# Row turns ahead of the projection's product groups, two chunks of the feed-forward interleaved, and an earlier fetch of tile ends

## What is computed

```python
agg = jax.ops.segment_sum(w[:, :, None] * v[srcidx], tgt, num_segments=n)
attn = agg.reshape(n, D) @ Wo[l].T + bo[l]
x = _batchnorm(x + attn, g1[l], beta1[l])
ff = jax.nn.relu(x @ W1[l].T + b1[l]) @ W2[l].T + b2[l]
x = _batchnorm(x + ff, g2[l], beta2[l])
```

## Time and profile before

| | us |
|---|---|
| median of 3 runs | 3085.25 |
| lowest and highest | 3076.72 and 3087.95 |
| span of the profiled execution | 3095.6 |
| PE busy in it | 2657.9 (86%) |
| DVE busy in it | 1629.2 (53%) |
| granted clock of PE, mean | 0.938 |

### The profile page before, as it was taken

The page is one execution under the profiler, slowest core; times in us unless marked ns, Lnnn a source line. Parts: engine busy times, 40 slices in busy tenths (PEclk is TensorE's granted clock), DMA queues, the critical chain, the costliest instruction groups (busy, mean ns, idle before and its releaser), DMA issues.

```text
span 3095.6 us, 78344 instructions
## 1 busy us (share of the span) xinstructions
PE 2657.9 (86%) x32605; PEld 2143.5 (69%) x32605; DVE 1629.2 (53%) x3272; ACT 1321.1 (43%) x3690; POOL 1115.8 (36%) x1130
## 2 busy tenths in 40 slices
PE   5999997999999999758899788888888678599998
PEld 4877885777777777546488577777777465477777
DVE  5236785555555555456512355555554645656553
ACT  3324443555555555422232255555555322333432
POOL 0000002666666666400001267777777111222110
PEclk8999998999999999979999899999999889799998
DMA  5642003988899998641024489999999431122211
GB/s 195 228 175 107 31 28 140 317 313 316 309 331 322 317 325 297 222 121 41 14 97 154 160 321 354 352 349 347 350 347 352 126 113 57 38 89 92 69 59 58
DMA packets 231795, 621.75 MB, mean 201 GB/s; under 512 B 39008, under 2 KB 45792, under 8 KB 231427
## 3 DMA queue, kind: packets, MB, share of 16 engines
q0 software_dynamic: 137088, 466.78, 42.2%
q1 hardware_dynamic: 94339, 149.78, 14.6%
HBM read 538.80 MB, written 103.39 MB: 207 GB/s over the span
## 4 chain that ended last, share of the span: by engine, by line
PE 60%; DMA 16%; DVE 8%; POOL 7%; issue 6%; ACT 2%; SPq 0%; DVEq 0%; POOLq 0%; ACTq 0%
PE ps L1179 6%; DMA Y<-KVd,srcE 5%; PE ps L574 5%; PE ps L575 4%; PE ps L576 4%; DMA aggd<-stage,segs 4%; PE ps L1222 4%; PE ps L1209 4%; PE ps L774 3%; POOL Y L1096 3%; PE ps L942 2%; PE ps L944 2%; PE ps L943 2%; PE ps L1186 2%; PE ps L1872 2%
## 5 line engine op out<-in xcount | busy, mean ns | idle before, releaser
L1096 POOL DMA_INDIRECT Y<-KVd,srcE x449 | 430.2, 958 | 230.6 <-issue 115.8
L1370 ACT ACTIVATE stage<-ps,stage 128x128 f32<-128x128 f32 x832 | 294.8, 366 | 115.3 <-PE ps L1186 112.4
L1096 POOL DMA_INDIRECT WA<-KVd,srcE x186 | 179.3, 964 | 361.8 <-PE ps L576 268.1
L1351 ACT ACTIVATE work<-ps 128x512 f32<-128x512 f32 x309 | 179.8, 597 | 303.8 <-PE ps L1179 303.5
L1179 PE MATMUL ps<-ident,Y 128*128 128x128 f32 x1796 | 252.2, 280 | 32.2 <-DMA Y<-KVd,srcE 26.8
L1351 ACT ACTIVATE G<-ps 128x512 f32<-128x512 f32 x315 | 181.8, 597 | 223.5 <-PE ps L1179 223.1
L1277 DVE COPY G<-ps 128x512 f32<-128x512 f32 x208 | 143.8, 691 | 245.8 <-PE ps L1186 243.0
L574 PE MATMUL ps<-Wh,xs 128*128 128x512 f32 x600 | 238.7, 398 | 31.2 <-DVE xs L514 31.2
L1179 PEld LDWEIGHTS ps<-ident,Y 128*128 128x128 f32 x1796 | 199.2, 143 | 70.5 <-issue 49.3
L575 PE MATMUL ps<-Wl,xs 128*128 128x512 f32 x600 | 236.9, 395 | 0.0
L576 PE MATMUL ps<-Wh,xs 128*128 128x512 f32 x600 | 236.5, 394 | 0.0
(11 more groups left out here) (383 smaller groups left out, 6775.2 us busy)
## 6 DMA issues: line engine op xcount, KB each, us to landing
KVd<-stage SPq DMA_DIRECT2D x96, 256.0 KB, 2.0
aggd<-work SPq DMA_DIRECT2D x6, 2048.0 KB, 7.4
Qd<-stage SPq DMA_DIRECT2D x48, 256.0 KB, 2.0
G<-aggd SPq DMA_DIRECT2D x48, 256.0 KB, 2.7
Y<-KVd,srcE POOLq DMA_INDIRECT x449
Y<-in_x SPq DMA_DIRECT2D x4, 1536.0 KB, 14.7
G<-mixq SPq DMA_DIRECT2D x24, 256.0 KB
mixd<-rowsb SPq DMA_DIRECT2D x24, 256.0 KB
```

Of the source, the lines that this page charges most:

```text
L1096: pool.indirect_dma_start(out=kvs[a], out_offset=None, in_=KVd[l][:, :], in_offset=bass.IndirectOffsetOnAxis(ap=srcE[:, n:n + 1], axis=0)) ...
L1351: act.activation(kT[n % len(kT)], banks(l)[place_of(l, "k", n) % len(banks(l))][:, :], ACT.Copy).then_inc(out_a, 1)
L1370: last = act.activation(pT[g % len(pT)][:, P * i:P * (i + 1)], SC[g % 2][:, P * i:P * (i + 1)], ACT.Exp, bias=smin[:, t:t + 1], scale=-1.0 ...
```

## The change

In the output projection the turn of a row of the next chunk, and its low part on DVE, stand ahead of a product group and no longer behind it. In the feed-forward PE's order becomes the list `FF_ORDER`: hidden layer 0, then for each chunk the first output block, the hidden layer of the next chunk, and the other three output blocks; the banks follow that list. The fetch of the tile ends waits only for the last use of the buffer that it overwrites (slot 18 in the first layer, 0 in the second), and the wait for the end of the edge phase comes behind it.

```diff
+        ENDS_KV = (18, 0)
+
         def ends_sp(l):
-            edges_done(sp, l)
+            a = ENDS_KV[l]
+            sp.wait_ge(agg, NQ * l + (KVN[l] * (uses(ET, KVN[l], a) - 1) + a) // 4 + 1)
...
             sp.dma_start(ends, src).then_inc(ends_in, 16)
+            edges_done(sp, l)
...
+        FF_ORDER = [(0, 0)]
+        for c in range(NCK):
+            FF_ORDER += [(c, 1), (c + 1, 0)] if c + 1 < NCK else [(c, 1)]
+            FF_ORDER += [(c, i) for i in range(2, 5)]
+
+        def ff_bank(c, i):
+            return FF_ORDER.index((c, i)) % 4
...
                 for f in range(4):
+                    if c + 1 < NCK and f < len(NODE_TILES[c + 1]):
+                        turn_row(NODE_TILES[c + 1][f])
                     if c:
...
                     mm.then_inc(wo_mm, 1)
-                    if c + 1 < NCK and f < len(NODE_TILES[c + 1]):
-                        turn_row(NODE_TILES[c + 1][f])
...
+            for c, i in FF_ORDER:
+                c0, cn = CHUNKS[c]
+                bank, o = PS[ff_bank(c, i)], FF_ORDER.index((c, i)) - 4
+                if o < 0:
+                    pe.wait_ge(wo_add, WO * (l + 1))
+                else:
+                    before, part = FF_ORDER[o]
+                    if part == 0:
+                        pe.wait_ge(relu, NCK * l + before + 1)
                     else:
+                        pe.wait_ge(ff_add, WO * l + 4 * before + part)
+                if i == 0:
+                    is_normal(pe, 2 * l, c)
...
                     i = WO * l + 4 * c + f + 1
+                    if c + 1 < NCK and f < len(NODE_TILES[c + 1]):
+                        low_row(NODE_TILES[c + 1][f])
                     dve.wait_ge(wo_mm, i)
...
                     dve.bn_stats(out=st4[:, f, c, :], in_=xT[:, f, c0:c0 + cn]).then_inc(*step_v.up())
-                    if c + 1 < NCK and f < len(NODE_TILES[c + 1]):
-                        low_row(NODE_TILES[c + 1][f])
```

More of the change, by code:

```diff
@@ L1875, in finish_pe @@
                     mm.then_inc(wo_mm, 1)
-                    if c + 1 < NCK and f < len(NODE_TILES[c + 1]):
-                        turn_row(NODE_TILES[c + 1][f])
[L1878 to L1885, removed]
-                    else:
[L1887 to L1897, removed]
+            for c, i in FF_ORDER:
[7 more added lines that the diff above has]
+                        pe.wait_ge(relu, NCK * l + before + 1)
+                    else:
+                        pe.wait_ge(ff_add, WO * l + 4 * before + part)
+                if i == 0:
+                    is_normal(pe, 2 * l, c)
+                    for k in range(4):
+                        mm = pe.matmul(bank[:, 0:cn], W1[:, k, :], xT[:, k, c0:c0 + cn], start=(k == 0), stop=(k == 3))
+                    mm.then_inc(w1_mm, 1)
+                else:
+                    if i == 1:
+                        pe.wait_ge(relu, NCK * l + c + 1)
+                    pe.matmul(bank[:, 0:cn], W2[:, (i - 1) * P:i * P], work[:, c % 3, 0:cn], start=True, stop=True
+                              ).then_inc(w2_mm, 1)
         def finish_act(l, meanwhile, beside_ff):
@@ L1926, in finish_act @@
                     act.wait_ge(w2_mm, WO * l + 4 * (c - 2))
-                act.activation(work[:, c % 3, 0:cn], PS[5 * c % 4][:, 0:cn], ACT.Relu, bias=vec[:, C_B1 + l:C_B1 + l + 1]
+                act.activation(work[:, c % 3, 0:cn], PS[ff_bank(c, 0)][:, 0:cn], ACT.Relu, bias=vec[:, C_B1 + l:C_B1 + l + 1]
                                ).then_inc(relu, 1)
@@ L1997, in finish_dve @@
                         is_normal(dve, 2 * l, c)
-                    dve.scalar_tensor_tensor(out=xT[:, f, c0:c0 + cn], in0=PS[(5 * c + f + 1) % 4][:, 0:cn],
+                    dve.scalar_tensor_tensor(out=xT[:, f, c0:c0 + cn], in0=PS[ff_bank(c, f + 1)][:, 0:cn],
                                              scalar=vec[:, C_B2 + 4 * l + f:C_B2 + 4 * l + f + 1],
```

## The result

The changed kernel has a median of 3097.37 us over 15 runs (3085.58 to 3110.6), the kernel before 3081.19 us over 15 (3074.69 to 3093.23). The ratio is 1.0049, 95% interval 1.0036 to 1.0063: 15 us slower, between 11 and 19. The prediction said 3097, or 11.4 us more, in a range from 3083 to 3107. That 3097 and 3097.37 all but agree is partly luck: the prediction's base, 3085.25 from three runs, lay 4 us above the median of 15, and the difference was 15 us where 11.4 was forecast.

A forecast was written before the change was run, and what follows sets the result against it. PE was taken to bound the kernel, with DVE close behind in the feed-forward. Projection -16.9, ring +18.6, clock +10.5 and tile ends -0.8 summed to +11.4 us on 3085.25, so 3097 us, range 3083 to 3107.

The forecast's parts named there:

- Row turns ahead: Output projection: turning rows ahead of product groups removes PE's waits for DVE's low parts; -16.9 us in both layers.
- Ten stops: Output projection, both layers: PE's 1.73 us stops at chunks' first groups all vanish, 17.3 us gained.
- one wait new: Output projection, first layer: PE waits for row 6's fetch at its turn; 0.4 us taken, bounds 0 and 2.8.
- The ring: Feed-forward: hidden layer, block 2, three DVE adds, normalisation, next hidden layer; 9.84 us a chunk instead of 7.97, +18.6 us.
- the relu is hidden by the interleaving: Feed-forward: next chunk's relu runs during three output blocks; alone it would save 0.87 us for each of six chunks a layer.
- The clock: Feed-forward: stops of 2.8 us drop PE to 1.2 GHz; seven of ten at 1.5 us, +10.5, bounds 0 and 17.
- The tile ends: After the edge phase: earlier fetch lets DVE start 0.8 us sooner in the second layer, nothing gained in the first.
- The sum: Whole kernel: the four terms together, +11.4 us, from 3085.25 to 3097 us.

The follow-up runs named there:

- e1: Kernel before with only the row turns and DVE's low parts ahead of the product groups; ratio 0.9932 against the kernel before.
- e9: Changed kernel with unread products, three a stop (two ahead of the last hidden layer), filling PE's stops; ratio 1.0015 against the kernel before.
- e6: Changed kernel with the next chunk's hidden layer behind the second output block instead of the first; ratio 0.9968 against the kernel before.
- e7: Changed kernel with the next chunk's hidden layer behind the third output block, one block left behind it; ratio 0.9955 against the kernel before.
- e4: Changed kernel with DVE normalising chunk c+2 behind its first add of chunk c instead of c+1's ahead of it; ratio 0.9925 against the kernel before.
- e2: Kernel before with only the interleaved order of the feed-forward's products; ratio 1.0093 against the kernel before.
- e3: Kernel before with only the tile ends fetched at the last use of their buffer; ratio 1.0002 against the kernel before.
- e8: Kernel before, all three edits absent, with only DVE's normalisation of chunk c+2 moved behind its first add of chunk c; ratio 0.9995 against it.

## Why the prediction was right

**Row turns ahead: right.** Ten stops gone, one wait new, in the place named. It was the term's size that was off in the changed kernel: 1.57 us for row 6 where I took 0.4 between bounds of 0 and 2.8. In e1 it was 0.7, with 0.3 in the second layer. In the first layers of the other kernels with this edit the wait lies anywhere from 0.4 to 2.0 us, so it depends on how late the fetch behind the weight loads lands in that execution. Measured: the stage of the first layer went from 98.50 to 92.0 (from the turn of row 4, which now stands ahead of the first product, at 1368.02, to 1460.02), of the second from 97.97 to 88.7 (2497.32 to 2586.06), 15.7 against 16.9 predicted.

**The ring: right.** 9.84 us predicted, 9.81 measured where the clock held; stops of 2.71 against 2.8; 0.10 from the normalisation to PE against 0.05. e9 gives the ring's cost without the clock: 67.6 + 68.7 - 59.0 - 59.2 = 18.1 us, where 18.6 was predicted. e6 and e7 confirm the same sum with one and with two adds less in it, and e4, which takes the normalisation out, ends it. That the relu is hidden by the interleaving was right too, and its 0.87 us a chunk was there to be had, but only with the ring open.

**The clock: right in kind, too high in number for the profiled run.** I took seven of ten stops at 1.5 us. In the changed kernel four brought it down, at 1.4 to 1.7 each; in e2 six of ten, one at 3.1. So it cost 24.0 - 18.1 = 6 us in the changed kernel's profile, 12 in e2's (30.3 - 18.1), 10 by the ratios (e9 against the changed kernel), and the 10.5 of the prediction lies among them. How many stops do it differs between the two profiled executions that share this feed-forward. The kernel that the Trainium skill tells of ("TensorE: Matmul & The Clock Gate", HAM oscillation) waited longer in each pass than PE does here; that each of the ten stops costs does not follow from it, and no run shows that.

**The tile ends: small as expected, but with the other sign.** The time from PE's first product behind the edge phase to DVE's first use of the ends:

```profile
1299.19 0.94 PE L1645 MATMUL ps<-ordE,ident 128*128 128x416 f32 x2 [0.86 <-PE ps L1222]
...
1312.71 0.58 DVE L1715 TENSOR_TENSOR Y<-mt 8x417 f32<-8x417 int32 x1
...
2433.01 0.94 PE L1645 MATMUL ps<-ordE,ident 128*128 128x416 f32 x2 [0.86 <-PE ps L1222]
...
2441.98 0.58 DVE L1715 TENSOR_TENSOR Y<-mt 8x417 f32<-8x417 int32 x1 [6.12 <-issue]
```

In the second layer that is 8.97, and 8.67 and 9.99 in e4 and e3, against 9.53, 9.50 and 9.53 in the kernel before, e2 and e1: 0.3 sooner on average, where I expected 0.8, and DVE no longer waits for the transfer. In the first layer, where I expected nothing, it is 13.52, 13.39 and 13.59 with the early fetch and 11.93, 12.02 and 11.84 without: 1.6 later, in each of three kernels of either kind. Over all fourteen kernels the early fetch stands at 12.8 to 13.6 (ten) and the late one at 11.8 to 12.0 (four), 1.3 apart on average; in the second layer the averages are 9.4 and 9.5. What the prediction held fixed, POOL's release of the barrier, moved: it comes 6.60 to 7.38 us behind PE's first product with the early fetch and 5.99 to 6.15 with the late one, in both layers. In the second layer of the changed kernel DVE starts 2.37 behind the release, 2.69 predicted, but the release itself comes 0.6 later. In the trace of the changed kernel it is PE that passes the branch late, at 1308.82, 9.6 behind its first product; it was 7.4 before. SP now has the three weight loads issued 1.5 us behind the end of the edge phase; before, behind the fetch of the ends, it was at them for 7.0 us (4.18, 1.60 and 1.14). That PE's program is fetched beside these loads, and so later, is my reading; it was not tested, and the cause stays open. Net +1.3 us instead of -0.8 (+1.2 over all fourteen).

**The sum.** -15.7 + 24.0 + 1.3 = +9.6 us by the profiles of one execution each, +15 (11 to 19) by the runs. With e2's count of falls instead of the changed kernel's it would be +16. So the rest may be the number of stops that bring the clock down, which one profile cannot give; that was not measured over many executions, and the rest stays unexplained.

## What to carry over

An order that hides one wait of PE can close a ring through another engine. Before changing the order, walk from one hidden layer to the next through every engine and add up: if the sum is above each engine's own work, no engine is busy all the time and the ring sets the pace. Here moving one normalisation into an idle time of DVE turned +24 us into -7.5.

A stop costs more than its length when PE's clock falls in it. Stops of 1.33 and 1.73 us never brought it down here: the clock was 1.00 behind all 8 of e6 and behind all 40 of the kernel before, e2, e3 and e8. Stops of 2.71 did in 9 of 16, and one of 2.23 in 1 of 4. Filling them with products that nobody reads was worth 10 us.

Work on POOL is not free for DVE only because it has a queue of its own. It doubled DVE's normalisation in e7, where that cost 0.94 us a chunk, and nearly doubled one in e4, where it cost PE nothing, because the normalisation was off the ring.

## Not expected of the hardware

- The fall of the clock is not the same behind stops of the same length: behind stops of 2.71 us the eight rows of a hidden layer took 3.67, 5.06 to 5.37, or 6.73 us.
- DVE's normalisation of two blocks takes 0.99 us alone and 1.99 to 2.07 beside POOL's subtractions in SBUF, which in turn take 2.69 instead of 2.49; DVE's adds from PSUM kept their 0.73 to 0.75 in the same places, and its statistics their 0.69.
- Behind the fetch of the ends (8 rows of 417 pairs) SP took 4.18, 1.60 and 1.14 us to issue three weight loads that it issues in 0.40, 0.50 and 0.49 without it. In both layers of the kernel before, e1, e2 and e8 the first of the three took 4.16 to 4.87; the other two varied from 0.50 to 2.25. Yet with the fetch moved away, DVE's first use of the ends in the first layer came 1.3 us later on average, in ten kernels against four.
